# Moving ScalarE's copy of the first turned queries ahead of the router's exponential, and turning the gate rows as 40 rows

## The chip, the core and the metric

The kernel runs on one core of one Trainium2 chip. The metric is the time of one execution on the device, in microseconds (us). Engines: PE is TensorE's matmul side, PEld its weight loads, DVE is VectorE, ACT is ScalarE, POOL is GpSimd, SP is SyncE. A difference under about 0.2% cannot be told from no change on this kernel.

## What is computed

The reference, cut to what matters. x and ctx are 32 x 512 x 512 in float32; there are 8 heads of 64 columns.

```
q = layernorm(x);  k = v = ctx
ig, fg = [q, k, v] @ igate_w.T + b, [q, k, v] @ fgate_w.T + b          # 8 gate rows each
csum = cumsum(log_sigmoid(fg))
log_D[s, t] = csum[s] - csum[t] + ig[t]   (t <= s);  D = exp(log_D - max_t log_D)
C = (q k^T / 8 + q . rpe[hops]) * D
h = C / (max(|sum C|, exp(-max log_D)) + 1e-6) @ v;  att = layernorm_per_head(h) * (1 + ln_w) + ln_b
x1 = x + att
n = layernorm(x1);  logits = n @ gate_w.T  (10 experts, top 2 kept, 8 of them true)
out = x1 + n @ base_w.T + base_b + 2 * sum_e weight_e * (n @ lora_A_e.T) @ lora_B_e.T
```

## The kernel before

A first phase of some 1,500 us makes the products of queries and position rows and stores them in DRAM. The change does not touch it. The second phase, the rounds, takes the 32 batches one after another as a software pipeline that is written out by hand. In one round one batch is prepared (`rp`), the next older one goes through attention (`ra`), and two older ones go through the output layer (`rf`, then `rg` for what is left of its last tiles). A round has 12 steps, `s` = 0 to 11. Every engine runs its own function `run` with a loop over the steps, and in each step it issues what the tables of steps give to it. The order on an engine is the order of the code. Between engines there are only semaphores: `act_p.done(b, ("x", 0))` is ScalarE's count when the copy of query tile 0 of batch b is complete.

The parts that are spoken of below, with their lines in the profile:

- **Query tiles** (4 of 128 rows to a batch). DVE normalizes a tile (L1018), TensorE turns it by four 128x128 transposes into PSUM bank 6 (`turn`, L1296), and ScalarE copies the turned tile to SBUF (`queries`, L806). Tile 0 is turned in step 1, after `weigh(0)`.
- **Context tiles** are turned by the same `turn` and copied by ScalarE at L798.
- **Attention** per unit of work u (12 to a batch, one in each step): `scores` (L1349, L1357) on TensorE, `unit_decay` (L826) on ScalarE, a mask (L698 or L702) on POOL, the product (`unit_weights`, L1073) on DVE, and `weigh` (L1373) on TensorE.
- **The output layer** per tile t: POOL scales and adds (L713, L718, L723, L728), DVE adds and takes the statistics (L1204, L1207, L1209), ScalarE turns the variance into a factor (L748, L750), DVE normalizes (L1179), TensorE turns (L1296), and the router's matmul follows (L1424). The router on DVE is a chain of small instructions. It takes the gap of the two best logits (L1142), waits for ScalarE's exponential of the gap (L886), goes on with L1147, L1150, L1153, L1155, L1157 and L1159, and ends with `mix` (L1162).
- `base(r, t)` on TensorE: two 128x512 matmuls (each is two MATMUL rows in the trace, L1406), then the transpose of `mix` (L1390), then two more of L1406, then the matmul of the turned mix (L1408). It writes PSUM bank 6, so it waits until bank 6 has been read. For tile 3 of `rg`, which comes due in step 2, that read is the copy of query tile 0:

```
if rp:
    read = (("x", 3), "gctx", "stats", ("x", 0))[t]
    pe.wait_ge(act_p.sem, act_p.done(rp.b, read))
```

- **Gate rows.** `g_rows` holds 8 rows (0 to 7) and 8 rows (32 to 39) of 512 columns, the others are zero. In step 10 TensorE turns it in four pieces (`gate_stats`), and ScalarE copies columns 0 to 39 of each turned piece (`statT`, L891).

In step 1 the router of tile 3 of `rg` is at work (ROUTE holds 13, which is step 1 of the round after). That happens in the 29 rounds in which both a batch is prepared and an `rg` exists.

Of the kernel before, what the change touches and what calls it, by code (L numbers as in the profile page):

```python
# [5 lines left out]
P = 128  # L6
# [91 lines left out]
def build(nc, x, ctxt, hops, igate_w, igate_b, fgate_w, fgate_b, rpe, ln_w, ln_b,  # L98
# [4 lines left out]
    KT = DIM // P  # L103
# [16 lines left out]
    GR = FG + NH  # L120
# [16 lines left out]
    with ExitStack() as ctx:  # L137
# [8 lines left out]
        def place(n):  # L146

            top[0] += n
            assert top[0] <= ARENA, top[0]
            return arena[:, top[0] - n:top[0]]  # L150

        def bank(n, width=BANK):
            return psum[:, n * BANK:n * BANK + width]


        ident = place(P)
# [69 lines left out]
        g_z, g_m, g_l, g_c, g_zi, g_rows, g_ctx = [place(S) for _ in range(7)]  # L226
# [108 lines left out]
        X_NORM, X_TURN = [0, 2, 3, 4], [1, 3, 4, 5]  # L335
# [13 lines left out]
        def at_step(table, s):  # L349
            return [t for t in tiles if table[t] == s]  # L350
# [36 lines left out]
        pe_p = Stage(sem("pe_p"), pe_p_steps)  # L387
# [357 lines left out]
        def _(act):  # L745
# [28 lines left out]
            for n in range(GROUPS):  # L774
# [12 lines left out]
                s, c, k = GROUP[n]  # L787
# [5 lines left out]
            def run(rn, rp, ra, rf, rg):  # L793
# [8 lines left out]
                def queries(t):  # L802
                    act.wait_ge(pe_p.sem, pe_p.done(rp.b, ("x", t)))
                    if t == 0:
                        act.wait_ge(pe_a.sem, pe_a.done(rp.b, ("score", UNITS - 1), 2))
                    nc.scalar.copy(qT[rp.par][:, :, t * P:(t + 1) * P],  # L806
                                   bank(6).rearrange("p (k s) -> p k s", k=KT)).then_inc(
                        act_p.sem, act_p.step(("x", t)))
# [40 lines left out]
                for s in range(STEPS):  # L849
                    if rp and s == X_TURN[ST - 1]:  # L850
                        queries(ST - 1)
                    if ra and s + 1 < UNITS:
                        unit_decay(ra, s + 1)
                    for t, r in due(TURN, s, rf, rg):
                        act.wait_ge(*dve_f.at(r.b, ("mean", t)))
                        rstd(act_f, r.b, ("ln", t), ("rstd", t), f_stats[:, 7:8], f_stats[:, 7:8])
                    for t in at_step(X_NORM, s):
                        if rp and t:
                            root(t)
                    if rf and s == 0:  # L860
                        pair_turned(rf, 3)
                    if rp and s == X_NORM[0]:
                        root(0)
                    for t in at_step(C_TURN, s):
                        if rp:
                            keys(t)
                    for t in at_step(X_TURN, s):
                        if rp and 0 < t < ST - 1:
                            queries(t)
                    if rf and s == 1:  # L870
                        act.wait_ge(dve_o.sem, dve_o.done(rf.b, "var_all"))
                        act.wait_ge(*pool_f.at(rf.b, ("scale", ST - 1), 1))
                        nc.scalar.activation(head_rs, head_rs, ACT.Ln).then_inc(act_n.sem, act_n.step("head_ln"))
                        act.wait_ge(act_n.sem, act_n.done(rf.b, "head_ln"))
                        nc.scalar.activation(head_rs, head_rs, ACT.Exp, scale=-0.5).then_inc(
                            act_n.sem, act_n.step("head_rs"))
                    if rp and s == LOG:
                        act.wait_ge(dve_p.sem, dve_p.done(rp.b, "abs"))
                        nc.scalar.activation(g_l[0:NH, :], g_l[0:NH, :], ACT.Exp, scale=-1.0).then_inc(
                            act_p.sem, act_p.step("exp"))  # L880
                        act.wait_ge(act_p.sem, act_p.done(rp.b, "exp"))
                        nc.scalar.activation(g_l[0:NH, :], g_l[0:NH, :], ACT.Ln, bias=1.0).then_inc(
                            act_p.sem, act_p.step("ln"))
                    for t, r in due(ROUTE, s, rf, rg):
                        act.wait_ge(*dve_f.at(r.b, ("gap", t)))
                        nc.scalar.activation(route[:, 2:3], route[:, 2:3], ACT.Exp).then_inc(*act_f.inc(("exp", t)))  # L886
                    if rp and s == STATS:
                        act.wait_ge(pe_p.sem, pe_p.done(rp.b, "stats"))
                        act.wait_ge(act_a.sem, act_a.done(rp.b, ("exp", UNITS - 1), 2))
                        act.wait_ge(dve_o.sem, dve_o.done(rp.b, "pos", 2))  # L890
                        nc.scalar.copy(statT[rp.par],  # L891
                                       bank(6).rearrange("p (t s) -> p t s", t=ST)[:, :, 0:GR]).then_inc(
                            act_p.sem, act_p.step("stats"))
                    if rp and s == GATES:
                        act.wait_ge(pe_p.sem, pe_p.done(rp.b, "gates"))
                        act.wait_ge(dve_p.sem, dve_p.done(rp.b, "a", 1))
                        nc.scalar.copy(g_ctx[0:GR, :], bank(6)[2 * FG:2 * FG + GR, :]).then_inc(
                            act_p.sem, act_p.step("gctx"))
                    if ra and s in TURNED:
                        pair_turned(ra, TURNED.index(s))  # L900
                    if ra and s in BACK:
                        pair_out(ra, BACK.index(s))
                    if rf and s == 0:
                        pair_out(rf, 3)
                    for t in at_step(X_TURN, s):
                        if rp and not t:
                            queries(t)
                    for t, r in due(BASE, s, rf, rg):
                        act.wait_ge(*pe_f.at(r.b, ("mix", t)))
                        act.wait_ge(*pe_f.at(r.b, ("base", (t - 1) % ST), 1 if t < 1 else 0))  # L910
                        nc.scalar.copy(mixT, bank(7)[:, MIX_AT:MIX_AT + P]).then_inc(*act_f.inc(("mixT", t)))
                    for t, r in due(TURN, s, rf, rg):
                        act.wait_ge(*pe_f.at(r.b, ("turn", t)))
                        act.wait_ge(*pe_f.at(r.b, ("base", (t - 2) % ST), 1 if t < 2 else 0))
                        nc.scalar.copy(ffn_xT[t % 2].rearrange("p k s -> p (k s)"), bank(7)).then_inc(
                            *act_f.inc(("xT", t)))
                    if rp and s == FLOOR:
                        act.wait_ge(dve_p.sem, dve_p.done(rp.b, "maxlog"))
                        act.wait_ge(pe_p.sem, pe_p.done(rp.b, "stats", 1))
                        nc.scalar.activation(g_rows[FG:GR, :], g_c[0:NH, :], ACT.Exp, scale=-1.0).then_inc(  # L920
                            act_p.sem, act_p.step("floor"))
                    if rp and s == STEPS - 1:
                        unit_decay(rp, 0)
# [293 lines left out]
        def _(pe):  # L1217
# [6 lines left out]
            for n, (srcs, rows_in, cols, dst, scale, split) in enumerate(jobs):  # L1224
# [4 lines left out]
                for i, src in enumerate(srcs):  # L1229
                    last = nc.tensor.transpose(bank(n % 8)[:, i * cols:(i + 1) * cols], src,  # L1230
                                               ident[0:rows_in, 0:rows_in])
# [3 lines left out]
            def queries(g):  # L1235
                pe.wait_ge(dve_q.sem, dve_q.done(g, "norm"))
                pe.wait_ge(act_q.sem, act_q.done(g, "copy", 1))
                for k in range(KT):
                    last = nc.tensor.transpose(bank(QUERY_BANK)[:, k * P:(k + 1) * P], x_norm[:, k * P:(k + 1) * P], ident)
                last.then_inc(pe_q.sem, pe_q.step("turn"))  # L1240
# [10 lines left out]
            for n in range(GROUPS):  # L1251
                s, c, k = GROUP[n]
                width = hop_width(n)
                qt = q_turned[n % 2].rearrange("p (k v b) -> p k v b", k=KT, v=VG)
                for o in hop_order(n):
# [10 lines left out]
                    if o[0] != "prod":  # L1266
                        copied(bank_before(o))
                        for q in range(KT):
                            last = nc.tensor.transpose(turn_bank(o)[:, q * P:(q + 1) * P],  # L1269
                                                       own[:, q * P:(q + 1) * P], ident)  # L1270
# [22 lines left out]
            def run(rn, rp, ra, rf, rg):  # L1293
                def turn(b, src):
                    for k in range(KT):
                        last = nc.tensor.transpose(bank(b)[:, k * P:(k + 1) * P], src[:, k * P:(k + 1) * P], ident)  # L1296
                    return last
# [33 lines left out]
                def gate_stats():  # L1331
                    pe.wait_ge(dve_p.sem, dve_p.done(rp.b, "a"))
                    pe.wait_ge(act_p.sem, act_p.done(rp.b, "floor"))
                    if rf:
                        pe.wait_ge(*dve_f.at(rf.b, ("out", 1)))
                    turn(6, g_rows).then_inc(pe_p.sem, pe_p.step("stats"))

                def scores(u):

# [143 lines left out]
```

## Time and profile before

| | |
|---|---|
| three runs | 3703.38, 3699.72 and 3701.87 us, median 3701.87 |
| the profiled execution, own time | 3707.81 us |
| its span, first to last instruction | 3706.1 us |
| mean granted TensorE clock, share of full speed | 0.944; 1.00 in the rounds |
| instructions | 70399 |
| busy: PE, DVE, ACT, POOL | 87%, 72%, 48%, 55% |

The profiled execution is one sample, and 0.16% above the median. A row of the timeline gives the start, the duration and how many instructions were merged; in brackets stands how long the engine was idle before it and what ended that. Starts of consecutive matmuls are closer together than their durations, since they are pipelined. One round takes 67.25 us.

### The profile page before, as it was taken

How to read it: one execution, taken by the hardware profiler on the slowest of the kernel's cores; microseconds unless marked ns; L12 is line 12 of the kernel's file. 1: busy time of each engine (PE TensorE's matmuls, PEld its weight loads, DVE VectorE, ACT ScalarE, POOL GpSimd, SP SyncE). 2: the span in 40 equal slices, each digit the busy share in tenths (PEclk: the TensorE clock that was granted, in tenths of full speed). 3: DMA queues.
4: the chain of work that ended last, by engine and by line, in shares of the span. 5: the costliest groups of instructions: out<-in, count | busy, mean ns of one | idle time of the engine just before them, and what ended most of it. 6: DMA issues, size and time to landing. Idle time of an engine off the chain costs nothing.

```text
span 3706.1 us, 70399 instructions
## 1 busy us (share of the span) xinstructions
PE 3237.0 (87%) x24884; PEld 1904.7 (51%) x24884; DVE 2667.8 (72%) x5497; ACT 1768.3 (48%) x4225; POOL 2031.3 (55%) x2248
## 2 busy tenths in 40 slices
PE   5777777777777777699999999999999999999997
PEld 4454454544445444355555555555555555555554
DVE  5455555555555555588888889888888898888885
ACT  2444444444444444455555555555555555555552
POOL 5677777777777776244444444444444444444443
PEclk8888888898998899799999999999999999999999
DMA  8999999999999998655555555555555555555541
GB/s 254 315 315 316 318 318 316 317 320 317 333 322 327 325 323 287 190 151 169 160 152 173 152 170 157 155 168 161 156 169 156 166 157 156 167 161 158 166 141 50
DMA packets 409680, 814.16 MB, mean 220 GB/s; under 512 B 100314, under 2 KB 204762, under 8 KB 407284
## 3 DMA queue, kind: packets, MB, share of 16 engines
q1 hardware_dynamic: 303860, 453.05, 39.7%
q0 software_dynamic: 87040, 285.28, 23.5%
q10 hardware_dynamic: 18432, 71.31, 5.1%
q8 instruction: 203, 3.33, 0.4%
q14 instruction: 145, 1.19, 0.1%
HBM read 632.67 MB, written 176.69 MB: 218 GB/s over the span
## 4 chain that ended last, share of the span: by engine, by line
PE 58%; DMA 15%; POOL 9%; DVE 9%; issue 6%; ACT 3%; SPq 0%; DVEq 0%; ACTq 0%
DMA arena<-in_L_xattn_rpe_dram,arena 15%; PE psum L1406 12%; PE psum L1349 7%; PE psum L1357 7%; PE psum L1269 7%; PE psum L1373 7%; POOL arena L683 7%; PE psum L1296 6%; PE psum L1285 3%; PE psum L1327 3%; PE psum L1408 3%; PE psum L1424 3%; POOL arena L674 2%; DVE arena L1179 1%; DVE arena L1073 1%
## 5 line engine op out<-in xcount | busy, mean ns | idle before, releaser
L1269 PE MATMUL psum<-arena 128*128 128x128 f32 x4352 | 691.5, 309 | 254.6 <-DMA arena<-in_L_xattn_rpe_dram,arena 237.5
L683 POOL DMA_INDIRECT arena<-in_L_xattn_rpe_dram,arena x768 | 728.7, 949 | 270.9 <-issue 181.8
L1269 PEld LDWEIGHTS psum<-arena 128*128 128x128 f32 x4352 | 545.3, 157 | 516.3 <-DMA arena<-in_L_xattn_rpe_dram,arena 357.7
L702 POOL TENSOR_SCALAR_AFFINE_SELECT arena<-arena 128x256 f32<-128x256 f32 x256 | 105.2, 411 | 746.9 <-ACT arena L826 644.4
L1406 PE MATMUL psum<-arena 128*128 128x512 f32 x1024 | 489.9, 608 | 22.0 <-ACT arena L806 22.0
L826 ACT ACTIVATE arena<-arena 128x512 f32<-128x512 f32 (+3 forms) x1024 | 503.4, 559 | 6.1 <-DMA arena<-gate_rows 5.3
L513 DVE COPY arena<-psum 128x512 f32<-128x512 f32 x384 | 263.3, 688 | 303.4 <-PE psum L1269 299.5
L1073 DVE TENSOR_TENSOR arena<-psum,arena 128x1024 f32<-128x1024 f32 (+1 forms) x384 | 397.5, 1041 | 37.6 <-PE psum L1357 31.1
L522 DVE COPY arena<-psum 128x416 f32<-128x416 f32 (+15 forms) x512 | 224.7, 441 | 266.8 <-PE psum L1285 261.1
L1285 PE MATMUL psum<-arena 64*32 64x416 f32 (+7 forms) x8192 | 370.6, 431 | 30.1 <-ACT arena L750 15.9
L674 POOL DMA_INDIRECT arena<-in_L_xattn_rpe_dram,arena x320 | 304.3, 951 | 165.0 <-issue 75.9
L1349 PE MATMUL psum<-arena 64*128 64x512 f32 (+3 forms) x2048 | 382.7, 471 | 0.0
L1357 PE MATMUL psum<-arena 128*128 128x128 f32 x2560 | 365.1, 282 | 0.0
L1296 PE MATMUL psum<-arena 128*128 128x128 f32 x2176 | 326.4, 283 | 43.4 <-DMA arena<-in_ctx_dram 12.0
L1373 PE MATMUL psum<-arena 128*64 128x512 f32 (+3 forms) x2048 | 359.6, 450 | 1.7 <-DVE arena L1073 1.5
L513 ACT COPY arena<-psum 128x512 f32<-128x512 f32 x384 | 224.4, 588 | 281.4 <-PE psum L1269 278.1
L522 ACT COPY arena<-psum 128x416 f32<-128x416 f32 (+15 forms) x512 | 199.1, 389 | 326.3 <-PE psum L1285 319.6
L1357 PEld LDWEIGHTS psum<-arena 128*128 128x128 f32 x2560 | 274.0, 141 | 155.9 <-issue 140.6
L1296 PEld LDWEIGHTS psum<-arena 128*128 128x128 f32 x2176 | 241.5, 142 | 198.0 <-issue 135.1
L1406 PEld LDWEIGHTS psum<-arena 128*128 128x128 f32 x1024 | 176.1, 192 | 199.0 <-issue 162.0
L1349 PEld LDWEIGHTS psum<-arena 64*128 64x128 f32 x2048 | 166.3, 186 | 161.1 <-issue 128.2
L748 ACT ACTIVATE arena<-arena 128x1 f32<-128x1 f32 x384 | 111.4, 290 | 274.4 <-DVE arena L978 150.2
(104 smaller groups left out, 4772.4 us busy)
## 6 DMA issues: line engine op xcount, KB each, us to landing
arena<-in_x_dram SPq DMA_DIRECT2D x256, 256.0 KB, 3.3
arena<-gate_rows SPq DMA_DIRECT2D x128, 512.0 KB, 4.6
arena<-in_x_dram SPq DMA_DIRECT2D x512, 64.0 KB
arena<-in_ctx_dram SPq DMA_DIRECT2D x32, 1024.0 KB, 7.7
out_dram<-arena SPq DMA_DIRECT2D x128, 256.0 KB, 2.3
arena<-in_L_xattn_rpe_dram,arena POOLq DMA_INDIRECT x1088
arena<-hop_products SPq DMA_DIRECT2D x128, 128.0 KB, 2.6
arena<-hop_products SPq DMA_DIRECT2D x128, 120.0 KB, 2.6
```

The source lines that it names most:

```text
L513: copy(rowsT[c % 2][:, o[2], :, o[3] * P:(o[3] + 1) * P], turn_bank(o).rearrange("p (k m) -> p k m", k=KT)).then_inc(*line.inc(o))
L522: copy(hop_out[c][:, lo:lo + width], bank(3 + 2 * (v % 2) + i, width)).then_inc(*line.inc(o))
L683: nc.gpsimd.indirect_dma_start(out=rows[v][:, t, :], out_offset=None, in_=rpe[:, :], in_offset=bass.IndirectOffsetOnAxis(ap=here[:, t, v:v ...
L826: last = nc.scalar.activation(decay[u % 3][:, e, at:at + width], top_pair[p % 2][:, e * S + j * P:e * S + j * P + width], ACT.Exp, bias=st ...
L1073: nc.vector.tensor_tensor(scoresT[u % 2][:, :, 0:width], got[:, :, 0:width], decay[u % 3][:, :, 0:width], ALU.mult).then_inc(dve_a.sem, dv ...
L1269: last = nc.tensor.transpose(turn_bank(o)[:, q * P:(q + 1) * P], own[:, q * P:(q + 1) * P], ident)
L1285: last = nc.tensor.matmul(psum[p * B:(p + 1) * B, at:at + width], qt[half, p, v, :], rowsT[c % 2][half, v, p, 0:width], start=True, stop=True)
L1296: last = nc.tensor.transpose(bank(b)[:, k * P:(k + 1) * P], src[:, k * P:(k + 1) * P], ident)
L1349: nc.tensor.matmul(psum[:, at[e] + col:at[e] + col + width], kT[ra.par][half, p, j * P:(j + 1) * P], qT[ra.par][half, p, j * P:j * P + width],
L1357: last = nc.tensor.matmul(psum[:, at[e] + n * P:at[e] + (n + 1) * P], hop_in[p % 2][:, e, Q_OFF[i] + j * P:Q_OFF[i] + (j + 1) * P], ident, ...
L1373: last = nc.tensor.matmul(psum[e * DH:(e + 1) * DH, 4 * BANK + j * P:4 * BANK + j * P + width], values[ra.par][:, j, HPT * p + e, :], scor ...
L1406: nc.tensor.matmul(bank(6), ffn_xT[t % 2][:, k, :], base_wT[:, k, :], start=(k == 0), stop=False)
```

## The change

Two edits. On ScalarE the copy of query tile 0 (`queries(0)`, step 1) is issued ahead of the router's exponential of that step, where it stood behind it. On TensorE the four transposes of the gate rows take 40 rows and write 40 columns, where they took 128 rows and wrote 128 columns.

```diff
@@ scalar, run
                         nc.scalar.activation(head_rs, head_rs, ACT.Exp, scale=-0.5).then_inc(
                             act_n.sem, act_n.step("head_rs"))
+                    if rp and s == X_TURN[0]:
+                        queries(0)
                     if rp and s == LOG:
...
                     if rf and s == 0:
                         pair_out(rf, 3)
-                    for t in at_step(X_TURN, s):
-                        if rp and not t:
-                            queries(t)
                     for t, r in due(BASE, s, rf, rg):
@@ tensor, gate_stats
                         pe.wait_ge(*dve_f.at(rf.b, ("out", 1)))
-                    turn(6, g_rows).then_inc(pe_p.sem, pe_p.step("stats"))
+                    for k in range(KT):
+                        last = nc.tensor.transpose(bank(6)[:, k * P:k * P + GR], g_rows[0:GR, k * P:(k + 1) * P],
+                                                   ident[0:GR, 0:GR])
+                    last.then_inc(pe_p.sem, pe_p.step("stats"))
```

ScalarE's instructions in steps 1 and 2 of a round in the middle, first before and then after the change. L873 and L875 make the factors of the heads, L886 is the exponential (L888 after the change, since lines have moved), L806 the copy of query tile 0, L826 belongs to step 2.

```order
2566 L798 ACTIVATE arena<-psum 128x4x128
2567 L873 ACTIVATE arena<-arena 128x32
2568 L875 ACTIVATE arena<-arena 128x32
2569 L886 ACTIVATE arena<-arena 128x1
2570 L806 COPY arena<-psum 128x4x128
2571 L826 ACTIVATE arena<-arena 128x512 x2
```

```order
2566 L798 ACTIVATE arena<-psum 128x4x128
2567 L873 ACTIVATE arena<-arena 128x32
2568 L875 ACTIVATE arena<-arena 128x32
2569 L806 COPY arena<-psum 128x4x128
2570 L888 ACTIVATE arena<-arena 128x1
2571 L826 ACTIVATE arena<-arena 128x512 x2
```

The copy and the exponential have changed places, and nothing else on ScalarE has moved. TensorE's instructions in step 10, before and after: the router's matmul (L1424, then L1426), the transposes of the gate rows (L1296, then L1336), and `weigh` (L1373, then L1375).

```order
2158 L1357 MATMUL psum<-arena 128x128 x8
2159 L1424 MATMUL psum<-arena 128x138 x4
2160 L1296 MATMUL psum<-arena 128x128 x4
2161 L1373 MATMUL psum<-arena 64x512 x2
2162 L1296 MATMUL psum<-arena 128x128 x4
```

```order
2158 L1359 MATMUL psum<-arena 128x128 x8
2159 L1426 MATMUL psum<-arena 128x138 x4
2160 L1336 MATMUL psum<-arena 128x40 x4
2161 L1375 MATMUL psum<-arena 64x512 x2
2162 L1295 MATMUL psum<-arena 128x128 x4
```

The order is the same, and the four transposes are narrower. The other engines have the same instructions in the same order.

## Rows read from the trace of the kernel before

**Rows 1.** Windows: length, busy PE, PEld, DVE, ACT, POOL, granted clock, DMA share, GB/s.

```profile
1644.10:3527.70 1883.60, 1857.79 (x10306) 1032.67 (x10305) 1662.75 (x3473) 998.39 (x2437) 872.99 (x1009) 1.00 0.53 161
```

**Rows 2.** Waits, 1620 to 3560 us: us in total, times, longest us.

```profile
DVE arena L1018 <- ACT arena L750: 37.6, 86, 0.6
...
PEld psum L1296 <- DVE arena L1179: 28.9, 58, 0.8
...
PE psum L1406 <- ACT arena L806: 22.0, 29, 0.9
```

**Rows 3.** Timeline of PE and PEld, steps 1 to 3 of one round.

```profile
2520.59 0.66 PE L1296 MATMUL psum<-arena 128*128 128x128 f32 x4
...
2523.41 0.65 PE L1296 MATMUL psum<-arena 128*128 128x128 f32 x4
...
2524.83 1.96 PE L1406 MATMUL psum<-arena 128*128 128x512 f32 x4 [0.76 <-ACT arena L806]
...
2526.62 0.27 PE L1390 MATMUL psum<-arena 128*128 128x128 f32 x1
...
2532.94 0.42 PEld L1296 LDWEIGHTS psum<-arena 128*128 128x128 f32 x4 [0.39 <-DVE arena L1179]
```

**Rows 4.** Timeline of ACT, the same round.

```profile
2524.01 0.20 ACT L886 ACTIVATE arena<-arena 128x1 f32<-128x1 f32 x1 [2.52 <-DVE arena L1142]
2524.11 0.57 ACT L806 COPY arena<-psum 128x512 f32<-128x512 f32 x1
2524.58 1.33 ACT L826 ACTIVATE arena<-arena 128x512 f32<-128x512 f32 x2
```

**Rows 5.** Timeline of DVE and POOL, the same round.

```profile
2525.49 0.23 DVE L1159 TENSOR_SCALAR arena<-arena 128x8 f32<-128x8 f32 x1
2525.76 0.29 DVE L1162 TENSOR_TENSOR arena<-psum,arena 128x128 f32<-128x128 f32 x1
...
2525.99 0.41 POOL L702 TENSOR_SCALAR_AFFINE_SELECT arena<-arena 128x256 f32<-128x256 f32 x1 [2.03 <-ACT arena L826]
...
2526.36 0.55 DVE L1018 TENSOR_SCALAR arena<-arena 128x512 f32<-128x512 f32 x1 [0.31 <-ACT arena L750]
...
2530.06 1.26 POOL L713 TENSOR_TENSOR arena<-arena 128x512 f32<-128x512 f32 x1
...
2531.79 0.55 DVE L1018 TENSOR_SCALAR arena<-arena 128x512 f32<-128x512 f32 x1 [0.40 <-ACT arena L750]
```

**Rows 6.** Timeline of step 2 in the one round that has no L806.

```profile
3598.36 0.20 ACT L886 ACTIVATE arena<-arena 128x1 f32<-128x1 f32 x1 [1.17 <-DVE arena L1142]
...
3599.72 0.23 DVE L1150 SCALAR_TENSOR_TENSOR arena<-arena 128x8 f32<-128x8 f32 x1
...
3599.86 0.41 POOL L702 TENSOR_SCALAR_AFFINE_SELECT arena<-arena 128x256 f32<-128x256 f32 x1 [0.20 <-ACT arena L826]
...
3600.83 0.29 DVE L1162 TENSOR_TENSOR arena<-psum,arena 128x128 f32<-128x128 f32 x1
3601.04 0.68 DVE L1073 TENSOR_TENSOR arena<-psum,arena 128x512 f32<-128x512 f32 x1
3601.18 0.14 PEld L1390 LDWEIGHTS psum<-arena 128*128 128x128 f32 x1 [1.15 <-DVE arena L1162]
```

**Rows 7.** Timeline of DVE and of POOL, step 11 of a round.

```profile
2573.79 1.30 DVE L1150 SCALAR_TENSOR_TENSOR arena<-arena 128x8 f32<-128x8 f32 x1
...
2573.80 1.27 POOL L728 TENSOR_TENSOR arena<-arena 128x512 f32<-128x512 f32 x1
```

**Rows 8.** Timeline of PE and PEld, step 10 of a round.

```profile
2569.48 1.11 PE L1424 MATMUL psum<-arena 128*128 128x138 f32 x8
...
2570.31 0.47 PEld L1296 LDWEIGHTS psum<-arena 128*128 128x128 f32 x4
...
2570.95 0.20 PEld L1373 LDWEIGHTS psum<-arena 128*64 128x64 f32 x4 [0.17 <-issue]
```

**Rows 9.** Timeline of PEld, the setup's eight transposes of 40 rows.

```profile
26.41 0.57 PEld L1230 LDWEIGHTS psum<-arena 40*128 40x128 f32 x8 [0.20 <-issue]
```

## The prediction

> **What bounds the kernel now.** I read the windows first, because the change touches only the rounds. Over 28 rounds PE is busy for 1857.79 of 1883.60 us at a granted clock of 1.00, DVE for 1662.75, ACT and POOL for about half [rows 1]. So TensorE's stream sets the pace, and its idle time is 25.8 us in 28 rounds, 0.92 us a round. An edit can pay in two ways: it takes work out of that stream, or it takes out idle time.
>
> The view of waits says where the idle time is. PE's base matmul (L1406) waits for ScalarE's copy L806 29 times, 22.0 us in all, once in each round with an `rg` [rows 2]. That is 0.76 us a round, most of the idle time. The first edit is aimed at it.
>
> The timeline shows how this wait comes about. Query tile 0 is turned by 2521.25 [rows 3]. ScalarE has then been idle for 2.52 us when the exponential starts at 2524.01, and only after that does it start the copy, at 2524.11 [rows 4]. The copy waits for nothing of its own, only for its place in the queue. PE has finished context tile 2 at 2524.06 and starts `base` at 2524.83 [rows 3].
>
> But another chain ends almost together with this one. The exponential releases the router on DVE, which ends in L1162 at 2526.05 [rows 5]. TensorE's transpose of the mix (L1390) starts at 2526.62 [rows 3]. So I must ask what is late next.
>
> **Edit 1, the copy ahead of the exponential.** It adds no instruction. The copy moves into ScalarE's idle 2.52 us: it would start at about 2521.5, and end at 2522.1. The exponential still starts at 2524.01, since it waits for DVE's L1142, and all on DVE up to there stays where it is. Then follows, step by step:
>
> (a) `base` starts when PE is free, at about 2524.0 in place of 2524.83. At this point 0.83 us are saved.
>
> (b) The transpose of the mix now meets L1162. In the last round the load L1390 waits 1.15 us and starts 0.05 us after L1162 ended, by the rounded rows 0.06 (3601.12 to 3601.18), and its matmul with it [rows 6]. With L1162 ending at 2526.05 the load could start at 2526.10. I allow 0.06 for a load that is not hidden, so the transpose counts as from 2526.16 in place of 2526.62, and PE gains 0.46 us in place of 0.83.
>
> (c) What follows on PE also waits for DVE. The turn of the next normalized tile loads at 2532.94, after 0.39 us idle behind L1179 [rows 3, 2]. So a gain on PE alone dies there: 0.46 would only make that idle time longer. What counts is how much earlier DVE gets to L1179. Between L1162 and L1179 DVE is dense but for two gaps. L1018 at 2526.36 waits 0.31 us for ScalarE's L750, which is late because the copy stood ahead of it. L1018 at 2531.79 waits 0.40 us for a chain that starts on DVE itself and moves with it [rows 5]. In the new order ScalarE starts L826 at 2524.11, 0.47 us earlier, and L750 too. The 0.31 goes, and 0.08 more, since an instruction of DVE that needs nothing of the one ahead starts before that one has ended: behind L1162 in the last round L1073 starts at 3601.04, and L1162 ends at 3601.12 [rows 6]. That is 0.39 us if L1162 itself stays.
>
> (d) L1162 may not stay. POOL's mask L702 starts 0.07 us behind L826. In the last round L702 starts 1.50 us after the exponential [rows 6]. In a changed round that is 2524.01 + 1.50 = 2525.51, where it was 2525.99 [rows 5]. DVE's L1159, a small TENSOR_SCALAR on SBUF, starts at 2525.49 and runs until 2525.72 [rows 5]. So POOL's start falls 0.01 to 0.03 us behind DVE's. Such a meeting is in the trace: L1150 starts at 2573.79 and POOL's L728 at 2573.80, and DVE's 0.23 us becomes 1.30, the time of POOL's instruction [rows 7]. The same meeting, at the same 0.01 to 0.02 us, is there 31 times, and DVE loses 31 times. Where DVE is ahead by 0.14 us neither is longer (3599.72 against 3599.86) [rows 6]. At 0.01 to 0.03 I expect POOL to win. L1159 would then end 0.03 us behind L702, at 2525.51 + 0.41 + 0.03 = 2525.95, 0.23 late. L1162 ends at 2526.28, L1390's load starts at 2526.33, and L1018 at 2526.20 in place of 2526.36.
>
> The Trainium skill (SBUF — State Buffer, Who interferes with whom) says that of VectorE and GpSimd the one that issues first gets the shared pair of ports. By that rule L1159 would win. The rows of L1150 and L728 contradict it at 0.01 us, and I follow them.
>
> So edit 1 gains 0.16 us where L1018 starts, and I add 0.02, an estimate, because L702 overlaps it no more (L1018's 0.55 starts inside L702's time now [rows 5]). On PE there are 0.23 us to gain, enough. 29 rounds x 0.18 = 5.3 us. The bounds are 0 (another wait takes all of it) and 29 x 0.39 = 11.3 us.
>
> **Edit 2, 40 rows instead of 128.** Four transposes a round stand in step 10 in a stretch where PE has no idle time. The four loads take 0.47 us, so one follows the other after (0.47 - 0.14) / 3 = 0.11 us [rows 8]. The setup has eight transposes of this very shape: eight loads in 0.57 us, one every (0.57 - 0.14) / 7 = 0.062 us [rows 9]. So 4 x 0.048 = 0.19 us is saved. Against this stands a change of shape. Before L1373 (128*64) the loads are idle for 0.17 us, while L1296 follows L1424, of the same 128*128 shape, with none [rows 8]. Before the 40-row loads of the setup the idle time is 0.20 us [rows 9]. L1373's load comes 0.31 us behind the last load of L1296, where 0.11 is usual. Of these 0.20 a load that runs ahead of its matmul hid 0.11, so the stream of matmuls loses 0.09 at such a change. The edit adds one, ahead of the four; the one behind is there already. 0.19 - 0.09 = 0.10, less 0.03 for a first load that nothing hides: 0.07 us a round, 32 rounds, 2.2 us. The bounds: no change of shape, 32 x 0.19 = 6.1 us gained; no faster stream and one change more, 32 x 0.09 = 2.9 us lost. The copy of the turned rows on ScalarE (L891) reads the same columns, and costs the same.
>
> The Trainium skill (TensorEngine Tiling (Array Packing), Key Properties) says that changing the tiling mode drains TensorE, and the idle 0.17 us agrees. It also says (TensorE: Matmul & The Clock Gate, LDWEIGHTS (loading the stationary operand)) that a load costs its columns alone, whatever the rows. By that rule the loads would take as long as now, and only the moving part would be shorter.
>
> **The sum.** 5.3 + 2.2 = 7.5 us. The profiled execution's own 3707.8 (span 3706.1) would become 3700.3. It stands 5.9 us above the median of the runs, which is 3701.87; taken from that: 3694.4 us.
>
> **The rivals.**
>
> - POOL's mask comes late enough, or DVE keeps its claim by being first, and L1159 is not held up. Then edit 1 gives 0.39 us a round: 11.3 + 2.2 = 13.5, 3688.4 us. For it: the last round, where 0.14 us of lead is enough. Against it: L1150 at 0.01 us. The point of decision lies between the two. Chance 0.22.
> - The wait only moves: L702 holds L1159, and the small rest of 0.18 us is lost in the next meeting of DVE and POOL or behind L1179. Then only edit 2 shows, 2.2 us or less, down to a loss of 2.9: 3699.7 us (up to 3704.8). For it: the chain over DVE is as long as PE's, and has changed by tenths. Against it: both gaps of L1018 are ScalarE's, and ScalarE gets ahead by 0.47. Chance 0.23.
> - Slower: DVE gets ahead of POOL by more than POOL follows, and L1018 at 2531.79 runs into POOL's L713. L713 ends at 2531.32, 0.47 us ahead of it [rows 5]. If DVE gained over 0.47 us on POOL there, a DVE instruction of 0.55 us would wait for one of 1.26. As for L1150 that may cost up to 1.07 us [rows 7]; 29 x 1.07 = 31 us, less the 7.5: 3725 us. At the gains of 0.18 or 0.39 it does not come to this. Chance 0.05.
>
> **How the numbers follow.** The forecast has 0.50: 3694.4, its own range 3690 to 3698. A measurement tells 0.2%, 7.4 us, from no change, and the forecast sits on that edge, so I give half of it to each side (0.26 faster, 0.24 same). With the first rival faster has 0.48, with the second same has 0.45 (0.02 of it beyond the edge), and slower has 0.07. The range takes in the first rival and most of the second: 3686 to 3702.
>
> **What the changed profile would show.** L806 starts at about 0.25 us behind L875, some 2.5 us ahead of the exponential. The wait of L1406 for L806 is gone, and the load L1390 has an idle time put down to L1162 instead. L702 starts 0.02 us behind L1159, and L1159 takes 0.46 us for tile 3 and 0.23 for the others, 0.29 in the mean. L1018 of step 2 has no idle time ahead of it. In step 10 the loads ahead of the four transposes are idle 0.15 to 0.2 us, and from the first L1424 to L1373's load it takes 0.07 us less. A round takes 67.00 us where it took 67.25. I would be wrong if L1159 keeps 0.23 us (a round of 66.8), or if a round stays above 67.1.

## The result and the profile after

Eight runs of the changed kernel have a median of 3691.26 us (3685.34 to 3694.76), eight of the kernel before 3701.64 us (3696.88 to 3707.67). The ratio is 0.9973, 95% interval 0.9963 to 0.9982: faster by 0.27%, where 0.20% was forecast. The profiled execution took 3691.55 us, with a span of 3689.8 us.

First the steady rounds, as the windows view gives them for 28 rounds (columns as in [rows 1]).

```profile
1638.00:3512.60 1874.60, 1855.06 (x10302) 1026.93 (x10301) 1662.51 (x3471) 998.37 (x2436) 874.28 (x1008) 1.00 0.54 162
```

28 rounds take 1874.6 us, where they took 1883.6 [rows 1]: 0.32 us a round less by these windows, 0.30 by the usual round (the median distance between one round and the next), which takes 66.95 us where it took 67.25. PE's idle time falls from 25.8 to 19.5 us. DVE does the same work.

The waits of the changed kernel (lines have moved: L1408 is `base`, L1392 the transpose of the mix, L1161 the mix on DVE, L1178 the normalization, L1017 the query tile's):

```profile
PEld psum L1392 <- DVE arena L1161: 52.6, 58, 1.5
...
DVE arena L1017 <- ACT arena L750: 29.0, 58, 0.6
...
PEld psum L1295 <- DVE arena L1178: 28.3, 57, 0.8
...
PE psum L1392 <- DVE arena L1161: 15.5, 29, 0.7
```

Of the three waits of PE and DVE that the prediction started from [rows 2], the one of `base` for the copy, 22.0 us, is gone. In its place stand 15.5 us of PE's matmul L1392 behind DVE's L1161, 0.53 a round. DVE's wait for L750 has lost one of its three cases a round (86 times, now 58). PEld's wait for L1178 (L1179 before) is what it was, 28.3 us for 28.9.

The timeline of the same place in the round, all engines:

```profile
2511.41 0.57 ACT L806 COPY arena<-psum 128x512 f32<-128x512 f32 x1
...
2513.92 1.88 PE L1408 MATMUL psum<-arena 128*128 128x512 f32 x4
2514.02 0.20 ACT L888 ACTIVATE arena<-arena 128x1 f32<-128x1 f32 x1 [2.04 <-DVE arena L1141]
2514.13 1.32 ACT L826 ACTIVATE arena<-arena 128x512 f32<-128x512 f32 x2
...
2515.51 0.44 DVE L1158 TENSOR_SCALAR arena<-arena 128x8 f32<-128x8 f32 x1
2515.52 0.41 POOL L702 TENSOR_SCALAR_AFFINE_SELECT arena<-arena 128x256 f32<-128x256 f32 x1 [1.55 <-ACT arena L826]
2515.99 0.29 DVE L1161 TENSOR_TENSOR arena<-psum,arena 128x128 f32<-128x128 f32 x1
2516.20 0.54 DVE L1017 TENSOR_SCALAR arena<-arena 128x512 f32<-128x512 f32 x1
2516.34 0.14 PEld L1392 LDWEIGHTS psum<-arena 128*128 128x128 f32 x1 [1.36 <-DVE arena L1161]
2516.34 0.33 PE L1392 MATMUL psum<-arena 128*128 128x128 f32 x1 [0.53 <-DVE arena L1161]
```

The copy runs 2.6 us ahead of the exponential, `base` follows PE's work without a wait, and POOL's mask L702 starts 0.01 us behind DVE's L1158 and holds it: 0.44 us, where the same instruction took 0.23 [rows 5]. PE's load follows L1161's end (2516.28) by 0.06.

Step 10, timeline of PE and PEld, to be held against [rows 8]:

```profile
2559.25 1.11 PE L1426 MATMUL psum<-arena 128*128 128x138 f32 x8
...
2560.29 0.32 PEld L1336 LDWEIGHTS psum<-arena 40*128 40x128 f32 x4
2560.66 0.20 PEld L1375 LDWEIGHTS psum<-arena 128*64 128x64 f32 x4
```

From the first L1426 (2559.25) to this load of L1375 it takes 1.41 us, where it took 1.47 from L1424 to L1373. The first load of 40 rows starts 0.07 us ahead of the end of the matmuls before it (2560.36).

### The profile page after: what moved, and what is told of

The parts are those of the page before. It is cut to its first block, busy times and chain, and to the rows that moved or that the text cites. A ratio compares the mean times of both kernels' runs of the same rounds, so it can differ in the third digit from the quotient of the medians.

```text
span 3689.8 us, 70399 instructions
## 1 busy us (share of the span) xinstructions
PE 3238.9 (88%) x24884; PEld 1901.0 (52%) x24884; DVE 2666.8 (72%) x5497; ACT 1768.2 (48%) x4225; POOL 2032.8 (55%) x2248
## 4 chain that ended last, share of the span: by engine, by line
PE 55%; DMA 15%; POOL 11%; DVE 10%; issue 6%; ACT 2%; SPq 0%; DVEq 0%; ACTq 0%; POOLq 0%
DMA arena<-in_L_xattn_rpe_dram,arena 14%; PE psum L1408 11%; POOL arena L683 8%; PE psum L1351 7%; PE psum L1359 7%; PE psum L1375 7%; PE psum L1268 6%; PE psum L1295 5%; PE psum L1326 3%; PE psum L1410 3%; PE psum L1284 3%; PE psum L1426 3%; POOL arena L674 3%; DVE arena L1178 1%; DVE arena L1072 1%
## 5 line engine op out<-in xcount | busy, mean ns | idle before, releaser
L1268 PE MATMUL psum<-arena 128*128 128x128 f32 x4352 | 695.9, 310 | 243.1 <-DMA arena<-in_L_xattn_rpe_dram,arena 225.2
L1268 PEld LDWEIGHTS psum<-arena 128*128 128x128 f32 x4352 | 547.2, 158 | 507.0 <-DMA arena<-in_L_xattn_rpe_dram,arena 356.6
L702 POOL TENSOR_SCALAR_AFFINE_SELECT arena<-arena 128x256 f32<-128x256 f32 x256 | 107.2, 419 | 731.3 <-ACT arena L826 628.9
L826 ACT ACTIVATE arena<-arena 128x512 f32<-128x512 f32 (+3 forms) x1024 | 503.0, 559 | 7.3 <-DMA arena<-gate_rows 6.5
L1408 PE MATMUL psum<-arena 128*128 128x512 f32 x1024 | 488.1, 604 | 0.0
L1359 PE MATMUL psum<-arena 128*128 128x128 f32 x2560 | 364.7, 282 | 0.0
L1375 PE MATMUL psum<-arena 128*64 128x512 f32 (+3 forms) x2048 | 359.2, 450 | 2.4 <-DVE arena L1072 2.3
L1359 PEld LDWEIGHTS psum<-arena 128*128 128x128 f32 x2560 | 273.6, 141 | 155.5 <-issue 140.1
L1295 PE MATMUL psum<-arena 128*128 128x128 f32 x2048 | 305.4, 282 | 34.4 <-DMA arena<-in_ctx_dram 11.9
L1295 PEld LDWEIGHTS psum<-arena 128*128 128x128 f32 x2048 | 225.3, 142 | 187.5 <-issue 134.6
L1408 PEld LDWEIGHTS psum<-arena 128*128 128x128 f32 x1024 | 177.3, 193 | 160.0 <-issue 152.1
L748 ACT ACTIVATE arena<-arena 128x1 f32<-128x1 f32 x384 | 111.3, 290 | 276.5 <-DVE arena L977 149.2
```

What stands on the lines that cost most here:

```text
L826: last = nc.scalar.activation(decay[u % 3][:, e, at:at + width], top_pair[p % 2][:, e * S + j * P:e * S + j * P + width], ACT.Exp, bias=st ...
L1359: last = nc.tensor.matmul(psum[:, at[e] + n * P:at[e] + (n + 1) * P], hop_in[p % 2][:, e, Q_OFF[i] + j * P:Q_OFF[i] + (j + 1) * P], ident, ...
L1375: last = nc.tensor.matmul(psum[e * DH:(e + 1) * DH, 4 * BANK + j * P:4 * BANK + j * P + width], values[ra.par][:, j, HPT * p + e, :], scor ...
L1408: nc.tensor.matmul(bank(6), ffn_xT[t % 2][:, k, :], base_wT[:, k, :], start=(k == 0), stop=False)
```

## The experiments

The sharpest measure is the length of a round, from one row of the trace: a DVE instruction that comes once a round (L1100 before), with the starts of its first and last execution. Two of these rows, before and after:

```profile
L1100 DVE TENSOR_SCALAR arena<-arena x28: 1187/1191/1198, 1644.1 to 3460.4; 128x32 f32<-128x32 f32 x28
```

```profile
L1099 DVE TENSOR_SCALAR arena<-arena x29: 1191/1196/1196, 1638.0 to 3513.1; 128x32 f32<-128x32 f32 x29
```

That is (3460.4 - 1644.1) / 27 = 67.27 us and (3513.1 - 1638.0) / 28 = 66.97. A few rounds of every kernel are 0.1 to 0.2 us longer, so this mean lies 0.02 to 0.03 above the usual round, which the expectations speak of.

| kernel | median, us | ratio to before, interval | mean round, us | usual round |
|---|---|---|---|---|
| before | 3701.1 to 3701.9 | | 67.27 | 67.25 |
| both edits | 3691.26 | 0.9973 (0.9963 to 0.9982) | 66.97 | 66.95 |
| e1, copy only | 3693.55 | 0.9978 (0.9968 to 0.9989) | 67.03 | 67.01 |
| e2, rows only | 3697.85 | 0.9985 (0.9976 to 0.9995) | 67.21 | 67.19 |
| e3, mask waits | 3687.15 | 0.9958 (0.9944 to 0.9972) | 66.76 | 66.73 |
| e4, 66 rows | 3688.04 | 0.9964 (0.9952 to 0.9976) | 66.84 | 66.82 |
| e5, factor early, old copy | 4186.15 | 0.9998 (0.9989 to 1.0007) | 67.29 | 67.27 |
| e6, factor early, new copy | 4169.24 | 0.9959 (0.9944 to 0.9974) | 66.78 | 66.75 |
| e7, 66 rows and mask waits | 4166.57 | 0.9954 (0.9940 to 0.9967) | 66.64 | 66.61 |

e5 to e7 ran on another chip, where the kernel before took 4183.47 us. Of the 480 us more, 478 lie ahead of the rounds: the row that comes at 1644.1 us before comes at 2122.2 in e5. That a round of the kernel before is as long on that chip was not profiled. It is inferred from e5, whose round is within 0.02 us of it and whose ratio is 0.9998. So e5 to e7 are compared by ratio and by round. The ratios are those on record; they are not quotients of the medians, and differ from these by up to 0.0008.

**e1, the first edit alone.** The diff is the first part of the change.

> The kernel before with the first edit alone (the copy of query tile 0 ahead of the exponential). My theory: what pays is that ScalarE reaches L750 earlier, so that DVE's L1018 of step 2 no longer waits, less the hold of L1159 by POOL's mask L702. A round should take 67.01 us (67.25 in the kernel before, 66.95 with both edits), in all 29 x 0.24 = 7.0 us less than before, about 3694.7. Rival: the removed wait of PE for the copy is worth its own 0.76 us; then a round takes 66.5 us and the kernel 22 us less. Second rival: most of the 0.30 us of both edits comes from the narrower transposes; then a round takes 67.1 us or more.

A usual round takes 67.01 us, as expected, and the kernel 3693.55 us. Both rivals fall: the copy gives 0.24 us of the 0.30, and not the 0.76 that PE waited. The size was right; that it comes through DVE's L1018, as the expectation says, is not shown by this, and e5 speaks against it.

**e2, the second edit alone.** The diff is the second part of the change.

> The kernel before with the second edit alone (the gate rows turned as 40 rows). My theory: 0.06 us a round, a round of 67.19 us, 1.9 us in all, about 3699.7, which a timing cannot tell from no change but the period of the rounds in the trace can. Wait of PE for L806 stays 0.7 to 0.8 us a round. Rival: without a cost for the change of shape 0.19 us a round, 67.06 us. Second rival: the gain is lost in the wait for the copy two steps later, 67.25 us.

The round takes 67.19 us: 0.06 us, as expected. 0.24 and 0.06 add up to the 0.30 of both. By the ratio the kernel is faster by 0.15% (0.05 to 0.24%), by the medians 3.2 us; the 1.9 us expected are 0.05%, at the edge of that interval. Both rivals fall (67.06 and 67.25). PE still waits for the copy (22.1 us, 29 times).

**e3, POOL's mask behind the mix.**

```diff
+                    if rg and ra and s == BASE[3] - STEPS:
+                        pool.wait_ge(*dve_f.at(rg.b, ("mix", 3)))
                     if ra and s + 1 < UNITS:
                         mask_future(ra, s + 1)
```

> Both edits, and POOL's mask of step 2 (L702) waits for the router's mix of tile 3 on DVE. Theory: L702 no longer holds up the router's last TENSOR_SCALAR (0.44 us back to 0.23), the mix ends 0.21 us earlier, and the round loses about 0.15 us more: 66.80 us, 29 x 0.15 = 4.4 us less than the changed kernel, about 3687. Rival: the 0.44 us have another cause than POOL's instruction; then it stays at 0.44 and the round at 66.95 us. Second rival: L702 now holds up L1018, which starts close to it, and a round takes 66.95 us or more.

The timeline of e3 (L1160 is the TENSOR_SCALAR, L1163 the mix, L1019 the query tile's):

```profile
2579.91 0.23 DVE L1160 TENSOR_SCALAR arena<-arena 128x8 f32<-128x8 f32 x1
2580.18 0.29 DVE L1163 TENSOR_TENSOR arena<-psum,arena 128x128 f32<-128x128 f32 x1
2580.38 0.54 DVE L1019 TENSOR_SCALAR arena<-arena 128x512 f32<-128x512 f32 x1
...
2580.52 0.33 PE L1394 MATMUL psum<-arena 128*128 128x128 f32 x1 [0.32 <-DVE arena L1163]
2580.54 0.64 POOL L702 TENSOR_SCALAR_AFFINE_SELECT arena<-arena 128x256 f32<-128x256 f32 x1 [2.17 <-DVE arena L1163]
```

With L702 out of the way the small instruction is back at 0.23 us, PE's wait falls from 0.53 to 0.32, and the round to 66.73: 0.22 less than with the change, where 0.15 was expected. So the hold by POOL is shown as the cause of 0.22 us, and all of it is on the path. Both rivals fall. Now DVE is 0.16 us ahead of POOL, and POOL's mask takes 0.64 us in place of 0.41; nobody waits for that.

**e4, 66 rows instead of 40.**

```diff
-                        last = nc.tensor.transpose(bank(6)[:, k * P:k * P + GR], g_rows[0:GR, k * P:(k + 1) * P],
-                                                   ident[0:GR, 0:GR])
+                        last = nc.tensor.transpose(bank(6)[:, k * P:k * P + 66], g_rows[0:66, k * P:(k + 1) * P],
+                                                   ident[0:66, 0:66])
```

> Both edits, but 66 rows of g_rows are turned in place of 40 (the rows above 39 are zero and are not read from the result). Theory: above 64 rows the shape of the weights is that of the router's matmul ahead (128 rows), so nothing idles ahead of the four; each costs (128 + 66) / 256 of 0.107 = 0.081 us. Against 128 rows 4 x 0.026 = 0.10 us is saved, against 40 rows 0.04: a round of 66.91 us. Rival: no cost of a change of shape, only the number of columns that stream; then 66 rows are slower than 40 by 4 x 0.02 = 0.08 us, 67.03 us.

The timeline of PE and PEld:

```profile
2619.78 1.11 PE L1426 MATMUL psum<-arena 128*128 128x138 f32 x8
...
2620.14 0.54 PEld L1426 LDWEIGHTS psum<-arena 128*128 128x128 f32 x4
2620.61 0.38 PEld L1336 LDWEIGHTS psum<-arena 66*128 66x128 f32 x4
2621.06 0.20 PEld L1375 LDWEIGHTS psum<-arena 128*64 128x64 f32 x4
```

More rows are faster: the round takes 66.82 us, 0.13 less than with 40 rows, where 0.04 was expected. The first load comes ahead of the end of the load before it (2620.14 + 0.54), as in [rows 8], and 0.28 us ahead of the end of the matmuls before it (2620.89), where the load of 40 rows came 0.07 ahead. From the first L1426 (2619.78) to L1375's load it takes 1.28 us, against 1.41 with 40 rows and 1.47 with 128. The rival is out: 40 rows pay for a change of shape that 66 rows do not, 0.13 us where 0.12 was reckoned (0.09 for the change and 0.03 for the first load, which no run tells apart). What was wrong in my numbers is the cost of a narrow transpose: with 66 rows the matmuls start 0.060 us apart, not 0.081, as close as with 40 rows (0.062).

**e5, DVE's factor early, the copy left where it was.** The kernel before, with ScalarE's L748 and L750 for query tile 1 ahead of the two L826 of step 2:

```diff
+                    if rp and s == X_NORM[1]:
+                        root(1)
                     if ra and s + 1 < UNITS:
                         unit_decay(ra, s + 1)
...
                     for t in at_step(X_NORM, s):
-                        if rp and t:
+                        if rp and t > 1:
                             root(t)
```

> The kernel before (the copy still behind the exponential, 128 rows turned), but in step 2 ScalarE computes the factor for L1018 (L748, L750 of query tile 1) ahead of the two L826. So DVE's L1018 waits no longer, and PE's wait for the copy stays. Theory on record in the prediction (DVE's chain from L1162 to L1179 decides): a round loses 0.31 to 0.45 us, 66.80 to 66.94 us. Rival, found in the trace since (PE's turn of the normalized tile started 0.07 us ahead of the end of the matmuls before it, as at every change of shape, so PE did not wait for DVE there): the stream of PE behind the transpose of the mix decides, DVE is some 0.1 us ahead of it, and the round stays at 67.25 us.

The timeline of e5 (L1408 is `base`, L1392 the transpose of the mix, L1020 is L1018 of before, L1181 the normalization, L1298 its turn):

```profile
3070.43 1.95 PE L1408 MATMUL psum<-arena 128*128 128x512 f32 x4 [0.76 <-ACT arena L806]
...
3071.56 0.54 DVE L1020 TENSOR_SCALAR arena<-arena 128x512 f32<-128x512 f32 x1
...
3072.22 0.27 PE L1392 MATMUL psum<-arena 128*128 128x128 f32 x1
...
3077.37 0.54 DVE L1181 TENSOR_SCALAR arena<-arena 128x512 f32<-128x512 f32 x1
...
3077.96 0.65 PE L1375 MATMUL psum<-arena 128*64 128x256 f32 x4
...
3078.54 0.42 PEld L1298 LDWEIGHTS psum<-arena 128*128 128x128 f32 x4 [0.39 <-issue]
```

DVE's L1020 behind the mix waits no more, and L1181 ends at 3077.91, 0.63 us ahead of the load L1298 (at least 0.45 in every round). The load still stands idle for 0.39 us and starts 0.07 us ahead of the end of the matmuls before it (3078.61). The round does not change. The theory on record, that DVE's chain to the normalization decides, has fallen.

The trace of the kernel before could have told it. Its rows of PE, PEld and DVE:

```profile
2512.13 0.65 PE L1373 MATMUL psum<-arena 128*64 128x256 f32 x4
2512.71 0.30 PEld L1349 LDWEIGHTS psum<-arena 64*128 64x128 f32 x4 [0.39 <-issue]
...
2532.25 0.54 DVE L1179 TENSOR_SCALAR arena<-arena 128x512 f32<-128x512 f32 x1
...
2532.36 0.65 PE L1373 MATMUL psum<-arena 128*64 128x256 f32 x4
...
2566.10 0.65 PE L1373 MATMUL psum<-arena 128*64 128x256 f32 x4
...
2566.89 0.42 PEld L1296 LDWEIGHTS psum<-arena 128*128 128x128 f32 x4 [0.60 <-DVE arena L1179]
```

The load at 2512.71 waits for nothing, and has the same 0.39 us idle ahead of it and the same 0.07 to the end of the matmuls (2512.78) as the load at 2532.94 ([rows 3], matmuls until 2533.01). L1179 had ended at 2532.79, 0.15 us before that load. The load at 2566.89 is another matter: it starts 0.14 us behind the matmuls' end, where 0.07 ahead is usual, and 0.05 behind L1179. There PE does wait for DVE, about 0.21 us in nearly every round. That idle time is 0.60 us in e5 too, as in all the runs, so the edits do not reach it.

**e6, the same with both edits.**

> Both edits, and in step 2 ScalarE computes the factor for L1018 ahead of the two L826, so that POOL's mask L702 starts 0.4 us later, at about the time at which L1018 starts. Theory: the router's TENSOR_SCALAR is free again (0.23 us) and the mix 0.21 us earlier, but POOL, 0.03 us ahead or close by, now holds L1018 for about 0.4 us (0.9 us in place of 0.54), so that PE meets a late L1179: a round of 66.95 to 67.05 us. Rival one, PE's stream alone decides: 66.73 us, as with the waiting mask. Rival two, DVE's L1018 keeps its time since it starts first: 66.73 us too, with L1018 at 0.54.

The timeline of e6 (L1160 is the router's TENSOR_SCALAR, L1019 the query tile's):

```profile
3065.47 0.23 DVE L1160 TENSOR_SCALAR arena<-arena 128x8 f32<-128x8 f32 x1
3065.90 0.41 POOL L702 TENSOR_SCALAR_AFFINE_SELECT arena<-arena 128x256 f32<-128x256 f32 x1 [1.97 <-ACT arena L826]
3065.95 0.65 DVE L1019 TENSOR_SCALAR arena<-arena 128x512 f32<-128x512 f32 x1
```

POOL starts first by 0.05 us, as expected, but the hold is 0.11 us (0.65 for 0.54) and not 0.4: DVE's instruction ends 0.29 us after POOL's. The round takes 66.75 us, as the first rival said. The normalization (L1180) now ends 0.06 us ahead of the load of its turn (3072.40 and 3072.46), where it was 0.15: the hold has used up what DVE was ahead there, and no more. So ScalarE's order alone, with no added wait, gives nearly what the waiting mask gives.

**e7, the two improvements together** (the edits of e3 and e4).

> Both edits with 66 rows in place of 40, and the mask of step 2 behind the mix: the two improvements found so far together. If they are independent, a round takes 66.73 - 0.13 = 66.60 us, 29 x 0.35 = 10 us less than the changed kernel, about 3681 us. If PE's gain in step 10 meets a later wait, 66.73 us.

66.61 us a round, as expected: 0.34 us less than the change, 29 x 0.34 = 9.9 us. The two add up. By the round it beats both kernels. By the times it is 0.46% faster than the kernel before (0.33 to 0.60%); it was not timed on one chip with the changed one.

## Why the prediction was right, point by point

- **What bounds the kernel, and where the wait is**: right. The wait for the copy was taken away, and it was worth 0.24 us of its 0.76 (e1).
- **(a) and (b)**, `base` starts when PE is free, then the transpose of the mix meets L1162: right. The new wait is 0.53 us a round, and the load follows the mix by 0.06 us.
- **(d)**, POOL's mask meets the small TENSOR_SCALAR and wins: right to 0.01 us (L702 forecast at 0.01 to 0.03 us behind, found at 0.01; 0.46 us forecast, 0.44 found), and shown by e3, and by e6, where L702 comes later for another reason and the small TENSOR_SCALAR is back at 0.23 us as well. That rule and rows differ was the point on which the forecast stood, and the rows were right.
- **(c)**, "a gain on PE alone dies there": wrong. The idle 0.39 us ahead of the turn at 2532.94 was put down to L1179 by the view of waits [rows 2, 3], and I took it for slack of PE. It is the idle of the loads at a change of shape, as before L1373 in [rows 8]. PE did not wait there. Its stream from the transpose of the mix onwards is the path, and DVE is some 0.1 us ahead of it at that load, so that its gap ahead of L1018 pays nothing (e5). That the size came out near is luck: DVE and PE both wait for L1162, and the wrong path gave 0.18 where the right one, in (b) and (d), has PE gain 0.46 - 0.23 = 0.23. Measured is 0.24. The changed kernel alone does not tell the two paths apart, since its L1178 still ends 0.15 us ahead of the load (2522.56 and 2522.71): DVE gained as much as PE. The term "29 x 0.18 = 5.3 us" (which works out at 5.2) is 29 x 0.24 = 7.0. For the same reason the first rival was priced at 0.39 and is worth 0.46, the gain of PE in (b): e3 has 0.24 + 0.22.
- **Edit 2**: 0.07 us forecast, 0.06 found (e2, and both together). That the change of shape takes most of it back is shown by e4. The idle time ahead of the four loads is 0.13 us (2560.16 to 2560.29), a little under the 0.15 to 0.2 forecast. Each load lasts 0.14 us with 40, 66 or 128 rows; what shrank is the distance between their starts.
- **The sum**: 0.25 us a round forecast, 0.30 found, 8.7 us over 29 rounds. The medians differ by 10.4 us, and the interval of the ratio (6.7 to 13.7 us) holds both. The spans differ by 16.3 us, but 6.1 of these are there when the first round that is counted starts (1644.1 against 1638.0), in a phase that the change does not touch, and which starts e1 to e4 at 1633 to 1640. One span is no measure of 9 us here; the length of a round is.

The second rival (only edit 2 shows) fell with e1. The slower one did not come about: POOL's L713 ends at 2521.09, 0.47 us ahead of DVE's L1017 at 2521.56, as far as before.

## What to carry to other kernels

A wait that is taken away is worth the distance to the next releaser: look up what else ends there, and price that, here a TENSOR_SCALAR of 0.23 us and the mask that an earlier ScalarE sets loose on it. An idle time that the view of waits puts down to another engine need not be a wait when the work ahead ends just then: compare the releaser's end with the start (here 0.15 us, where a load that did wait started 0.05 to 0.06 behind its releaser) before calling it slack. In a kernel of equal rounds, the length of a round settles tenths of a microsecond that the total cannot.

## What the runs showed of the hardware

- A TENSOR_SCALAR of DVE that starts 0.01 us ahead of a POOL instruction was held by it (0.44 us for 0.23, in all 28 such rounds of the changed kernel behind 1600 us), one that starts 0.16 us ahead held POOL (0.64 for 0.41). The Trainium skill (SBUF — State Buffer, Who interferes with whom) gives the ports, where the two contend, to whoever issues first. If the recorded starts stand for the order of issue, the first of these cases does not fit that, and the second does. Once in e5, at 2031.52, a TENSOR_SCALAR of 8x512 held L702 with a lead of 0.06 (0.61 for 0.41). The lead alone may not decide: at 2055.64 in e5 a SCALAR_TENSOR_TENSOR of 128x32 with a lead of 0.02 kept its 0.20 us.
- A held TENSOR_SCALAR of 128x512 loses less than the time of the POOL instruction that is left: 0.11 us where 0.36 were left (e6). It ended 0.29 us behind POOL's, where it takes 0.54 when nothing holds it.
- Between 128-row work, turning 66 rows is faster than turning 40, by 0.13 us for four. The first load of 40 rows starts 0.07 us ahead of the end of the matmuls before it, that of 66 rows 0.28 ahead. No run has a number of rows between these. The transposes themselves start 0.060 us apart with 66 rows, 0.062 with 40, and 0.11 with 128.
- At the changes between weights of 128*128, 64*128 and 128*64 where nothing is waited for, the load starts 0.07 us ahead of the end of the matmuls before it (2512.71 and 2532.94 before, 3078.54 in e5). So how long PEld stands idle follows from when those matmuls end: 0.17 us in [rows 8], 0.39 at 2532.94.
